# Router of the first three groups of a Flamingo block: one product in three 32-column strips of TensorE's array, and two transpositions of its result

## The reference, cut to what matters

```python
x = x + tanh(g_xattn) * attention(ctx, ctx, layernorm(x))
y = layernorm(x)
shared = (silu(y @ shared_w1) * (y @ shared_w2)) @ shared_w3
scores = sigmoid(y @ router_w)                      # 16 a token
_, top_idx = top_k(scores + expert_bias, 2)
gates = one_hot(top_idx).sum * scores               # 0 but for two experts
routed = sum over e of (silu(y @ w1[e]) * (y @ w2[e])) @ w3[e] * gates[:, e]
out = x + tanh(g_ffn) * (shared + routed)
```

## Time and profile before

| | us |
|---|---|
| median of three runs | 65.3 |
| lowest and highest of them | 64.07 and 66.3 |
| the profiled execution, its own time | 63.83 |
| span of the profiled execution, first to last instruction | 61.9 |
| PE busy | 55.1 (89%) |
| DVE busy | 42.7 (69%) |
| ACT busy | 23.8 (38%) |
| POOL busy | 19.1 (31%) |
| mean granted clock of TensorE | 0.978 |

### The profile page before, as it was taken

How to read it: one execution, slowest core, us unless ns; L and a number is a source line. 1 busy time by engine, 2 the same in 40 slices (tenths; PEclk the granted TensorE clock), 3 DMA queues, 4 the chain that set the end, 5 groups by cost and what they waited for, 6 DMA issues and landing times.

```text
span 61.9 us, 1259 instructions
## 1 busy us (share of the span) xinstructions
PE 55.1 (89%) x360; PEld 48.3 (78%) x360; DVE 42.7 (69%) x175; ACT 23.8 (38%) x74; POOL 19.1 (31%) x41
## 2 busy tenths in 40 slices
PE   0995899999999999999999999999999999999100
PEld 0313797998999999999999999999999997998000
DVE  3048979899859897883596989434876638887600
ACT  0623848859995133345322342222223322222000
POOL 4604299979049177680133500000000000000000
PEclk9999999999999999999999999999999999999965
DMA  0799970000000000000000054986720000002350
GB/s 0 184 257 296 364 306 4 0 0 0 0 16 0 0 0 0 0 0 5 0 0 0 0 141 130 282 236 211 196 86 0 0 5 0 0 11 85 94 166 11
DMA packets 5257, 4.77 MB, mean 77 GB/s; under 512 B 385, under 2 KB 5121, under 8 KB 5249
## 3 DMA queue, kind: packets, MB, share of 16 engines
q1 hardware_dynamic: 4816, 4.33, 22.8%
q10 hardware_dynamic: 432, 0.35, 2.4%
HBM read 4.15 MB, written 0.52 MB: 76 GB/s over the span
## 4 chain that ended last, share of the span: by engine, by line
PE 80%; DMA 5%; DVE 5%; issue 1%; POOL 1%; ACT 1%; DVEq 0%; POOLq 0%
PE bank L829 17%; PE bank L830 17%; PE bank L843 12%; DMA x_sb<-in_x_dram 5%; PE bank L856 4%; PE bank L810 3%; PE bank L987 3%; PE bank L797 3%; PE bank L978 3%; PE bank L790 3%; PE bank L977 3%; PE bank L785 3%; DVE final L636 2%; PE bank L822 2%; PE bank L816 2%; PE bank L780 2%
## 5 line engine op out<-in xcount | busy, mean ns | idle before, releaser
L415 ACT ACTIVATE silu_t<-bank 128x256 f32<-128x256 f32 x28 | 10.6, 383 | 24.8 <-PE bank L830 21.0
L608 DVE TENSOR_TENSOR hid<-silu_t,bank 128x256 f32<-128x256 f32 x28 | 11.3, 414 | 4.3 <-PE bank L843 2.7
L829 PE MATMUL bank<-x2nT,shared_sb 128*128 128x256 f32 x32 | 9.8, 387 | 0.0
L843 PE MATMUL bank<-shared_sb,hid 128*128 128x128 f32 x64 | 9.6, 276 | 0.0
L843 PEld LDWEIGHTS bank<-shared_sb,hid 128*128 128x128 f32 x64 | 9.2, 191 | 0.6
L830 PE MATMUL bank<-x2nT,shared_sb 128*128 128x256 f32 x32 | 9.5, 379 | 0.0
L830 PEld LDWEIGHTS bank<-x2nT,shared_sb 128*128 128x128 f32 x32 | 6.1, 190 | 0.8
L856 PE MATMUL bank<-tile_w,hid 128*128 128x128 f32 x32 | 4.8, 278 | 0.1
L829 PEld LDWEIGHTS bank<-x2nT,shared_sb 128*128 128x128 f32 x32 | 4.9, 192 | 0.0
L856 PEld LDWEIGHTS bank<-tile_w,hid 128*128 128x128 f32 x32 | 4.5, 191 | 0.4 <-issue 0.2
L324 POOL TENSOR_SCALAR x2n<-x,mean_var,rstd 128x128 f32<-128x128 f32 x6 | 4.7, 797 | 0.3
(11 more groups left out here) (117 smaller groups left out, 103.4 us busy)
## 6 DMA issues: line engine op xcount, KB each, us to landing
tile_w<-in_routed_w_dram SPq DMA_DIRECT2D x10, 192.0 KB, 4.5
shared_sb<-in_shared_w_dram SPq DMA_DIRECT2D x1, 768.0 KB, 6.1
out_dram<-final SPq DMA_DIRECT2D x4, 128.0 KB, 2.1
x_sb<-in_x_dram SPq DMA_DIRECT2D x2, 128.0 KB, 3.7
ctx_sb<-in_ctx_dram SPq DMA_DIRECT2D x2, 128.0 KB, 3.7
x_sb<-in_x_dram SPq DMA_DIRECT2D x1, 256.0 KB, 4.5
ctx_sb<-in_ctx_dram SPq DMA_DIRECT2D x1, 256.0 KB, 4.8
params<-in_attn_params_dram ACTq DMA_DIRECT2D x1, 201.0 KB, 3.0
```

Source lines behind the costliest of these rows:

```text
L415: nc.scalar.activation(silu_t[:, k % 3, :], bank[UP_BANK[k % 3]][:, 0:256], ACT.Silu).then_inc(silu_ready, 1)
L608: nc.vector.tensor_tensor(hid[:, k % 3, :], silu_t[:, k % 3, :], bank[UP_BANK[k % 3]][:, 256:512], ALU.mult)\
L829: nc.tensor.matmul(dst[:, 0:256], w1, x2nT[:, twos(g), :], start=True, stop=True)
L843: last = nc.tensor.matmul(dst[:, c * P:(c + 1) * P], hid[:, k % 3, i * P:(i + 1) * P], w3s[:, j, :], start=(j == 0 and c == 0), stop=(j == ...
```

## The change

The four routing calls become three pieces of work:

- `route_first`, after `share_up(7)`: the router's weights, widened with zeros to 32 columns (`rw_wide`), are the stationary operand, and the 256 tokens of a group the moving one. There is one such product for each of groups 0, 1 and 2, each in its own strip of 32 columns of the array (`tile_position=(0, 32 * g)`), and each writes its own 32 partitions of one bank.
- `turn_logits`, after `turn_x2(3)` and `share_down(5)`: ACT has copied the 96 by 256 result to `logitsT`, and PE turns it by two transpositions so that the tokens stand on the partitions.
- `route_last`, after `share_up(8)`: group 3 as before.

`squash_first` takes the tanh for the three first groups in one instruction. On DVE `choose(0)` moves behind `share(7)`, and `share(8)` goes between `choose(1)` and `choose(2)`. POOL gets a memset and a copy of the router's weights.

```diff
+        rw_wide = sb("rw_wide", [P, 32])
+        logitsT = sb("logitsT", [3 * 32, 256])
...
+            pool.memset(rw_wide[:, :], 0.0).then_inc(rw_ready, 1)
...
             add_bias(2)
+            pool.wait_ge(params_loaded, 16)
+            pool.wait_ge(rw_ready, 1)
+            pool.tensor_copy(rw_wide[:, 0:E], rw_sb).then_inc(rw_ready, 1)
...
-            def squash(g, src):
-                act.wait_ge(logits_done, g + 1)
-                nc.scalar.activation(th[:, twos(g), :], src[:, 0:2 * E].rearrange("p (b e) -> p b e", b=2), ACT.Tanh, scale=0.5)\
+            def copy_logits(src):
+                act.wait_ge(logitsT_done, 1)
+                nc.scalar.copy(logitsT[:, :], src[0:3 * 32, 0:256]).then_inc(logitsT_ready, 1)
+
+            def squash_first(src):
+                act.wait_ge(logits_done, 1)
+                nc.scalar.activation(th[:, 0:6, :].rearrange("p (g b) e -> p g b e", b=2),
+                                     src[:, 0:2 * 96].rearrange("p (b g e) -> p g b e", b=2, g=3)[:, :, :, 0:E], ACT.Tanh, scale=0.5)\
+                    .then_inc(th_ready, 3)
+
+            def squash_last(src):
+                act.wait_ge(logits_done, 2)
+                nc.scalar.activation(th[:, 6:8, :], src[:, 0:2 * E].rearrange("p (b e) -> p b e", b=2), ACT.Tanh, scale=0.5)\
                     .then_inc(th_ready, 1)
...
             silu(4)
-            squash(0, bank[3])
             silu(5)
             silu(6)
-            squash(1, bank[5])
             copy_x2(2, bank[0])
             silu(7)
+            copy_logits(bank[5])
             copy_x2(3, bank[2])
-            squash(2, bank[5])
+            squash_first(bank[3])
             silu(8)
-            squash(3, bank[0])
+            squash_last(bank[0])
...
             share(5)
+            share(6)
+            share(7)
             choose(0)
-            share(6)
             choose(1)
-            share(7)
+            share(8)
             choose(2)
             choose(3)
             mark()
-            share(8)
             share(9)
...
-            def route(g, dst):
-                pe.wait_ge(x2nT_ready, g + 1)
-                for i in range(2):
-                    last = nc.tensor.matmul(dst[:, i * E:(i + 1) * E], x2nT[:, 2 * g + i, :], rw_sb, start=True, stop=True)
+            def route_first(dst):
+                pe.wait_ge(rw_ready, 2)
+                pe.wait_ge(x2nT_ready, 3)
+                for g in range(3):
+                    last = nc.tensor.matmul(dst[32 * g:32 * g + 32, 0:256], rw_wide[:, :], x2nT[:, twos(g), :], start=True, stop=True,
+                                            tile_position=(0, 32 * g))
+                last.then_inc(logitsT_done, 1)
+
+            def turn_logits(dst):
+                pe.wait_ge(logitsT_ready, 1)
+                for i in range(2):
+                    last = nc.tensor.transpose(dst[:, i * 96:(i + 1) * 96], logitsT[:, i * P:(i + 1) * P], ident[0:96, 0:96])
+                last.then_inc(logits_done, 1)
+
+            def route_last(dst):
+                pe.wait_ge(x2nT_ready, G)
+                for i in range(2):
+                    last = nc.tensor.matmul(dst[:, i * E:(i + 1) * E], x2nT[:, 6 + i, :], rw_sb, start=True, stop=True)
                 last.then_inc(logits_done, 1)
...
             share_up(0)
-            pe.wait_ge(probs_ready, 6)
-            route(0, bank[3])
...
             share_up(6)
-            pe.wait_ge(x2_ready, 6)
-            route(1, bank[5])
             share_down(4)
             turn_x2(2, bank[0])
             share_up(7)
-            pe.wait_ge(th_ready, 2)
-            route(2, bank[5])
+            pe.wait_ge(x2_ready, 6)
+            route_first(bank[5])
             pe.wait_ge(x2_ready, 8)
             turn_x2(3, bank[2])
             share_down(5)
+            pe.wait_ge(probs_ready, 6)
+            turn_logits(bank[3])
             share_up(8)
-            route(3, bank[0])
+            route_last(bank[0])
             share_up(9)
```

More of the change, by code:

```diff
@@ L202, in flamingo_block @@
         x2nT_ready = sem("x2nT_ready")
+        rw_ready = sem("rw_ready")
+        logitsT_done = sem("logitsT_done")
+        logitsT_ready = sem("logitsT_ready")
         logits_done = sem("logits_done")
```

## The result

| | before | changed |
|---|---|---|
| median of six runs, us | 64.8 | 66.34 |
| lowest to highest, us | 64.07 to 66.3 | 65.08 to 67.44 |
| profiled execution, us | 63.83 | 65.52 |
| its span, us | 61.9 | 63.3 |

The ratio is 1.0205, with a 95% interval of 1.0157 to 1.0252: the change makes the kernel slower, by 1.6 to 2.5%; that it is more than 2% isn't settled. The forecast was +1.4 us or 2.1%. (The times of either version fall into two clusters some 1.7 us apart, and a ratio compares the faster cluster of one with the faster cluster of the other.)

The account below looks back on a forecast made before the run. PE (89% busy) bounds the kernel, but DVE's one-hot arrays, ready at 34.26 us, would start the counts 1.41 us later with nothing given back: median 65.3 becomes 66.7 us, 2.1% slower, range 65.1 to 68.4.

Parts of the forecast that it names:

- PE reaches `route_first` 0.90 us sooner: On PE, with two routing calls gone, route_first can start at 27.00 instead of 27.90 us.
- Strips, 1.30 us: On PE in route_first: three products of 256 columns, priced one after the other at 0.435 us each, 1.30 in all.
- PE's own balance, +0.22: PE's work: 1.30 us removed, 1.30 added by route_first and 0.22 by turn_logits, net +0.22 us.
- From the strips' end to `turn_logits`, 0.66: PE does turn_x2(3) and share_down(5), 0.22 + 0.44 us, covering the wait for ACT's copy with 0.05 to spare.
- The tanh starts 0.04 after the transpositions: Handover from PE to ACT: turned logits end at 29.34, squash_first starts at 29.38 and takes 0.25 us.
- VectorE's stretch, 4.59: On DVE from the first choose: four calls 3.76, share(8) 0.34, mark 0.49 us, together 4.59.
- Nothing is given back: Behind the counts: both sides shift by the same 1.41 us, and PE's own work bounds it to the end.
- Nothing outside the span: Whole execution: time goes 63.83 to 65.24 and span 61.9 to 63.3, both by the same +1.41 us.
- transpositions -0.05: On PE in turn_logits: the pair runs 0.38 us from start to end, from 28.96 to 29.34.
- strips one after another: Likeliest case, in route_first: products run in sequence, +1.2 to +1.6 us; chance 0.45.
- "side by side" rival: In route_first: strips overlap, taking 0.87 or 0.43 us; +0.98 or +0.54, median 66.3 or 65.8, within 2%; chance 0.27.
- The clock did not fall in the stall: Judges a rival at PE's wait before the counts: the clock falls during the stall; called unlikely, chance 0.04.

Follow-up runs that it names:

- squash_split: The changed kernel with the tanh of the first three groups in two instructions of 48 columns instead of one of 96; 66.30 us (one execution).
- strips_twice: The changed kernel with the three products of the strips done twice, 12 instructions instead of 6; 66.08 us (one execution).
- best_again: A second timing of the kernel best, unchanged; ratio to the kernel before 0.9975 (0.9877 to 1.0074), lowest 63.53 us.
- best: Changed kernel with choose over six blocks, tanh in two, share_up(11) and share_down(8) before the counts, three shares moved earlier on VectorE; lowest 63.23 us.

## Why the prediction was right, step by step

It named the place (the wait for VectorE's one-hot arrays ahead of the counts), the reason (all four calls of `choose` now lie behind the third group's logits) and the size, the last in part by luck. Its terms, against the trace after:

- **PE reaches `route_first` 0.90 us sooner.** Right: 27.07 is where it would start by `share_up(7)`'s distance, 27.00 was said, and `share_up(0)` began 0.07 later.
- **Strips, 1.30 us.** Wrong, the term that was mis-sized. From 27.07 to 27.73 the block took 0.66: 0.43 for the products, and 0.09 on entering and 0.14 on leaving, inside the 0 to 0.32 that had been bounded. The 0.09 and 0.14 are what is left over; nothing that PE waited for explains them, since the x2nT of the third group was there at 26.78 and the x2n of the fourth at 27.25. The nearest row, one product after another, was no guide to strips side by side. The Trainium skill's page TensorE: Matmul & The Clock Gate, Part 3, says that matmuls in different column strips run concurrently. The trace agrees, with 0.43 us for three products. The page's 2.38 is for 512 columns, and its table gives no data type; the estimate of 0.55 from it was nearer to the 0.66 of the block than 1.30 was. The Trainium skill's page TensorEngine Tiling (Array Packing), Key Properties, says that a change of the tiling mode drains TensorE. The 0.23 us for the two changes agree with that.
- **PE's own balance, +0.22.** Wrong with it: -0.39. PE came to the counts at 32.13 + 0.44 = 32.57, and so stood for 1.55 us and not 1.19.
- **From the strips' end to `turn_logits`, 0.66.** 0.72 (27.73 to 28.45), with no wait.
- **The tanh starts 0.04 after the transpositions.** Wrong: 0.42. The sum had the handover at 0.04 for every instruction, whatever its form. Its length, 0.25, was exact. squash_split shows that the form of the instruction was the cause.
- **VectorE's stretch, 4.59.** Right: 4.57. This was read from durations of before alone, and it is the term that made the forecast.
- **Nothing is given back.** Right: 22.77 us from the counts to the last group before, 22.78 after.
- **Nothing outside the span.** Wrong: the forecast moved time and span by the same 1.41 us, and the changed kernel has some 0.25 us more outside the span. No term stands for it.

The sum of the misses, on the ruler of `share_up(0)`: strips -0.64, way to `turn_logits` +0.06, transpositions -0.05 (0.33, not 0.38), tanh +0.38, three small ones 0.00, so -0.25; 1.41 - 0.25 = 1.16, as measured. Two misses of opposite sign made the total look better than its parts, and a third, outside the span, brought the time as measured back to the forecast: 1.16 + 0.25 = 1.41. That is luck. The case that the forecast stood on, strips one after another, isn't what happened. The case that did happen, side by side, had a chance of 0.27 and was forecast to stay within 2%. What holds without luck is the mechanism: the wait ahead of the counts, its releaser, and VectorE's 4.59 us. (The range's lower bound is added up wrongly by 0.1: 65.84 - 0.6 is 65.2.)

The "side by side" rival had the strips right and forecast +0.54 for it, because it lacked the tanh's 0.38 and the 0.23 for the two changes of the array's division. The clock did not fall in the stall: the granted clock of 33 to 35 us is 1.00. What remained of the difference in time (+1.69 us between the two profiled executions) is 0.07 ahead of `share_up(0)`, 0.17 in the stores behind VectorE's last group (57.85 against 56.62, so +1.23, where the span has +1.4), and 0.29 outside the span. The first two vary from run to run by as much; the third is the 0.25 that every run with the strips shows.

## What to carry to other kernels

Gathering small operations into a cheaper one moves the first result to where the last input is ready; look for a consumer on another engine that had used the time between, and add up its whole serial work from the new start before counting what is saved. Here 0.39 us of TensorE's time was saved and 1.55 us of waiting bought. Compare the time outside the span too, since no row shows it. If the gathered form is kept, let the consumer gather too (one `choose` over six blocks gave 0.94 us back), and move independent work of both engines into the gap, not of one alone.

## What the runs showed of the hardware

- **Three 128x32 float32 products with 256 columns each, in three column strips, took 0.43 us**, as one does in the whole array (strips_twice: 1.00 - 0.57). Beyond that the block took 0.09 us on entering and 0.14 on leaving.
- **An ACT instruction whose operands have three free dimensions began 0.38 us later** than its like with two (0.42 against 0.04 us after the release). No other form was tried.
- **VectorE's wait ahead of the first placed sum differed between two versions of its list**: 1.26 or 1.27 us in seven profiles, 0.91 us in the four with one `choose` over six blocks. The cause is open.
- **TensorE's pace in the first 10 us has two values.** In the profile of best_again PE worked at about half pace up to some 10 us: two instructions of 256 columns took 0.93 us to the next start (6.93 to 7.86), and 0.44 in the profile of the same kernel's first timing (6.59 to 7.03). PE had done the same before in both, seven products of a constant and two transpositions. This is nearly the whole of the 1.79 us between the starts of `share_up(0)` (17.75 against 15.96). Groups by line and shape of PE, 5.5 to 8 us, in best (busy us, mean ns of one, idle us before):

```profile
L805 PE MATMUL bank<-ctxT,kq 128*128 128x256 f32 x2 | 0.6, 380 | 0.0
L800 PE MATMUL bank<-ident,xn 128*128 128x128 f32 x2 | 0.4, 302 | 0.2 <-DVE xn L525 0.2
```

and in best_again, 6.8 to 10 us:

```profile
L805 PE MATMUL bank<-ctxT,kq 128*128 128x256 f32 x2 | 1.1, 672 | 0.0
L800 PE MATMUL bank<-ident,xn 128*128 128x128 f32 x2 | 0.6, 424 | 0.0
```

The granted clock is listed as 1.00 (2.4 GHz) in both for all of this stretch, though the products of best_again take about twice as long; so the row to look at is the products' own. squash_split, whose `share_up(0)` is at 17.69, has the same: two instructions of 256 columns took 1.02 us to the next start (7.18 to 8.20), with 1.00 granted. What slows them is not shown.
